# Attention units that hold two kinds of heads, in a kernel that puts attention beside a mixture of experts

## The reference

```
q, k, v = proj(xn): 16 heads of 8 numbers
idx   = clip(pos_k - pos_q, -20, 20) + 20
attn  = softmax((q.k + q.rel_k[idx]) / sqrt(8))         # 512 x 512 for each head and row
out   = (attn @ v + sum_k attn * rel_v[idx]) @ Wo.T + bo
```

## Time and profile before

| | |
|---|---|
| time, 3 runs | 2581.75, 2585.8, 2586.46 us (median 2585.8) |
| the profiled execution | 2584.21 us, its span 2582.4 us |
| attend in the span | from 282 us to 1671 us |
| busy in the whole span | PE 2293.3, DVE 1905.0, ACT 1584.7, POOL 1038.4 us |

### The profile page before, as it was taken

One profiled execution on the slowest core, in us unless ns is written; L12 is line 12 of the kernel. 1 busy time (PEld: TensorE's weight loads), 2 busy tenths in 40 slices (PEclk: granted clock), 3 DMA queues, 4 the chain that ended last, 5 costly groups with the idle time before them and its releaser, 6 DMA issues. The chain is left out here.

```text
span 2582.4 us, 102624 instructions
## 1 busy us (share of the span) xinstructions
PE 2293.3 (89%) x37544; PEld 1609.2 (62%) x37544; DVE 1905.0 (74%) x3734; ACT 1584.7 (61%) x3954; POOL 1038.4 (40%) x1350
## 2 busy tenths in 40 slices
PE   5773599999999999999998999869999996999999
PEld 3441477767767677677676777646666664666665
DVE  5663488878878788788787888637676764777777
ACT  3442477778777777777777777637777772232322
POOL 5664445545554555455445554300000002333332
PEclk9886799999999999999999999959999997999999
DMA  6887345544544455455444554300010101101010
GB/s 191 271 271 205 87 108 120 115 108 110 122 107 111 102 124 112 106 116 123 104 115 105 121 112 105 67 25 26 24 37 24 37 25 58 37 24 37 24 37 16
DMA packets 568188, 243.42 MB, mean 94 GB/s; under 512 B 462278, under 2 KB 531526, under 8 KB 563142
## 3 DMA queue, kind: packets, MB, share of 16 engines
q1 hardware_dynamic: 567750, 237.52, 36.7%
HBM read 134.13 MB, written 103.29 MB: 92 GB/s over the span
## 5 line engine op out<-in xcount | busy, mean ns | idle before, releaser
L886 ACT ACTIVATE a_probs<-a_bank_s,a_neg_max 128x512 f32<-128x512 f32 x1024 | 694.6, 684 | 184.2 <-DVE a_neg_max L821 180.1
L821 DVE TENSOR_REDUCE a_neg_max<-a_bank_s 128x2 f32<-128x1024 f32 x512 | 627.0, 1225 | 56.0 <-ACT a_probs L886 3.7
L673 PE MATMUL a_bank_pt<-a_ident,a_probs 128*128 128x128 f32 x4096 | 573.1, 283 | 8.5 <-issue 2.6
L673 PEld LDWEIGHTS a_bank_pt<-a_ident,a_probs 128*128 128x128 f32 x4096 | 445.1, 143 | 116.4 <-issue 79.1
L866 ACT ACTIVATE a_probs_t<-a_bank_pt 128x512 f32<-128x512 f32 x512 | 305.9, 597 | 201.4 <-PE a_bank_pt L673 196.0
L807 DVE COPY a_probs_t<-a_bank_pt 128x512 f32<-128x512 f32 x512 | 350.1, 684 | 32.4 <-PE a_bank_pt L673 24.5
L662 PE MATMUL a_bank_s<-a_k,a_q 48*32 48x512 bf16 (+15 forms) x4096 | 274.1, 290 | 94.0 <-DMA a_kl<-scr_parts 65.0
L699 PE MATMUL a_bank_o<-a_probs_t,a_v 128*32 128x32 f32 (+2 forms) x15872 | 305.8, 228 | 2.0 <-issue 2.0
L699 PEld LDWEIGHTS a_bank_o<-a_probs_t,a_v 128*32 128x32 f32 x15872 | 245.8, 112 | 58.8 <-ACT a_probs_t L866 48.4
L662 PE MATMUL a_bank_s<-a_kl,a_q 48*32 48x204 bf16 (+14 forms) x3840 | 241.4, 266 | 23.6 <-ACT a_probs L886 19.1
L800 DVE TENSOR_TENSOR a_bank_s<-a_bank_s,a_win 128x144 f32<-128x144 f32 (+2 forms) x640 | 164.2, 275 | 125.9 <-PE a_bank_s L662 113.1
(11 more groups left out here) (161 smaller groups left out, 3600.1 us busy)
## 6 DMA issues: line engine op xcount, KB each, us to landing
scr_probs<-a_probs SPq DMA_DIRECT2D x256, 144.0 KB, 5.2
a_raw<-scr_qr SPq DMA_DIRECT2D x256, 96.0 KB
scr_qr<-p_qr SPq DMA_DIRECT2D x64, 320.0 KB, 2.9
a_feat<-scr_probs SPq DMA_DIRECT2D x256, 78.0 KB
scr_parts<-p_sp SPq DMA_DIRECT2D x144, 128.0 KB, 2.9
a_left<-scr_probs SPq DMA_DIRECT2D x256, 64.0 KB, 2.5
a_q<-scr_parts SPq DMA_DIRECT2D x32, 192.0 KB
a_k<-scr_parts SPq DMA_DIRECT2D x32, 192.0 KB
```

What stands on the lines that cost most here:

```text
L673: ins = nc.tensor.transpose(b_pt[bank_of(job)][:, 0, t * P:(t + 1) * P], probs[(u - 1) % 4][:, j, MAX_REL + t * P:MAX_REL + (t + 1) * P], ...
L821: nc.vector.tensor_reduce(neg_max[:, 2 * pair:2 * pair + 2], b_s[:, 2 * pair:2 * pair + 2, :], AX.X, ALU.max, negate=True).then_inc(max_ok, 1)
L886: nc.scalar.activation(probs[u % 4][:, j, MAX_REL:MAX_REL + S], b_s[:, j, :], ACT.Exp, bias=neg_max[:, j:j + 1], accum_out=sums[:, t, j, u ...
```

## The change

In a unit, blocks 0 and 1 keep the heads u % 4, and blocks 2 and 3 take the heads u % 4 ^ 1, which have the other parity (`head_of`). The banks are reordered (`PLACES`): banks 0, 1, 2, 3 hold blocks 0, 2, 1, 3, so the two banks of a pair have heads of different parity. `scores` goes over both banks with `KL` and then over both with `K`; the number and the shapes of its matmuls stay. `attended` can no longer join blocks 1 and 2 in a part. `add_window`, the sums and the store follow the new places; the store of a unit becomes two stores of two blocks each (i = 0 and i = 2), and the waits on `p_out` count 32 instead of 16. The two units of a pair (u % 4 of 0 and 1, of 2 and 3) together still cover the same heads and blocks.

```diff
+PLACES = (0, 2, 1, 3)
+def head_of(u, i):
+    return u % 4 ^ i // 2
...
-                    sp.wait_ge(p_out[k], b * 16 * NT + 16 * (u // 4))
+                    sp.wait_ge(p_out[k], b * 32 * NT + 32 * (u // 4))
...
-                    at = PROBS_AT[t % 2] + u % 4 * NJ * QBLK * WIN
-                    own = probs[u % 4][:, 0, t * P:]
-                    sp.dma_start(bass.AP(scr["probs"].tensor, at, [[WIN, P], [H * QBLK * WIN, NQB], [1, WIN]]),
-                                 bass.AP(own.tensor, own.offset, [own.ap[0], [S + 2 * MAX_REL + QBLK, NQB], [1, WIN]])
-                                 ).then_inc(p_out[u % 4], 16)
+                    for i in (0, 2):
+                        at = PROBS_AT[t % 2] + (i * H + head_of(u, i) * NJ) * QBLK * WIN
+                        own = probs[u % 4][:, PLACES.index(i), t * P + i * QBLK:]
+                        sp.dma_start(bass.AP(scr["probs"].tensor, at, [[WIN, P], [H * QBLK * WIN, 2], [1, WIN]]),
+                                     bass.AP(own.tensor, own.offset,
+                                             [own.ap[0], [2 * (S + 2 * MAX_REL) + QBLK, 2], [1, WIN]])
+                                     ).then_inc(p_out[u % 4], 16)
...
-                par = slice((u % 2) * HALF, (u % 2) * HALF + ROWS)
-                for i in pair:
-                    at = u // 4 * P + i * QBLK
-                    edge = max(at - MAX_REL, 0)
-                    for keys, a, z in ((KL, 0, edge), (K, edge, S)):
+                for right in range(2):
+                    for p in pair:
+                        i = PLACES[p]
+                        at = u // 4 * P + i * QBLK
+                        edge = max(at - MAX_REL, 0)
+                        keys, a, z = (K, edge, S) if right else (KL, 0, edge)
                         if a == z:
                             continue
+                        par = head_of(u, i) % 2 * HALF
                         for g in range(NJ):
-                            half = (NJ * g + u % 4) // 2
-                            ins = nc.tensor.matmul(b_s[g * QBLK:(g + 1) * QBLK, i, a:z], Q[s][par, half, at:at + QBLK],
-                                                   keys[s][par, half, a:z], start=a == 0, stop=z == S,
+                            half = (NJ * g + head_of(u, i)) // 2
+                            ins = nc.tensor.matmul(b_s[g * QBLK:(g + 1) * QBLK, p, a:z],
+                                                   Q[s][par:par + ROWS, half, at:at + QBLK],
+                                                   keys[s][par:par + ROWS, half, a:z], start=a == 0, stop=z == S,
...
-                        parts = [(n * QBLK, (n + 1) * QBLK, EDGES.index(max(n * QBLK - MAX_REL, 0)))
-                                 for n in range(NQB)]
+                        parts = [(n, n + 1, EDGES.index(max(n * QBLK - MAX_REL, 0))) for n in range(NQB)]
                     elif kt == t - 1:
-                        parts = [(0, QBLK, EDGES.index(P - MAX_REL)), (QBLK, P, EDGES.index(P))]
+                        parts = [(0, 1, EDGES.index(P - MAX_REL)), (1, 2, EDGES.index(P)), (2, 4, EDGES.index(P))]
                     else:
-                        parts = [(0, P, EDGES.index(P if kt < t else 0))]
+                        parts = [(n, n + 2, EDGES.index(P if kt < t else 0)) for n in (0, 2)]
                     for lo, hi, edge in parts:
+                        p, hh = PLACES.index(lo), head_of(u, lo)
...
-                                                   probs_t[u % 2][:, lo // QBLK:hi // QBLK,
+                                                   probs_t[u % 2][:, p:p + 2 * (hi - lo) - 1:2,
                                                                   kt * P + j * QBLK:kt * P + (j + 1) * QBLK],
...
-                    near = bass.AP(whole.tensor, whole.offset, [whole.ap[0], [S + QBLK, n], [1, z - a]])
-                    ins = nc.vector.tensor_tensor(near, near, win[t % 2][:, i:i + n, hh, a - edge:z - edge], ALU.add)
+                    near = bass.AP(whole.tensor, whole.offset, [whole.ap[0], [S + 2 * QBLK, n], [1, z - a]])
+                    step = (2 * NJ + head_of(u, 2) - head_of(u, 0)) * WIN
+                    ins = nc.vector.tensor_tensor(near, near, bass.AP(own.tensor, own.offset, [own.ap[0], [step, n], [1, z - a]]),
+                                                  ALU.add)
```

More of the change, by code:

```diff
@@ L678, in attended @@
             def attended(b, u, s):
-                t, hh = u // 4, u % 4
+                t = u // 4
                 after = (b, u + 1) if u < UNITS - 1 else (b + 1, 0)
@@ L686, in attended @@
                     need(pe, o_ev, b, 1, 0)
-                first = hh == 0
+                first = u % 4 == 0
                 for kt in range(NT):
                     if kt == t:
-                        parts = [(n * QBLK, (n + 1) * QBLK, EDGES.index(max(n * QBLK - MAX_REL, 0)))
-                                 for n in range(NQB)]
+                        parts = [(n, n + 1, EDGES.index(max(n * QBLK - MAX_REL, 0))) for n in range(NQB)]
                     elif kt == t - 1:
-                        parts = [(0, QBLK, EDGES.index(P - MAX_REL)), (QBLK, P, EDGES.index(P))]
+                        parts = [(0, 1, EDGES.index(P - MAX_REL)), (1, 2, EDGES.index(P)), (2, 4, EDGES.index(P))]
                     else:
-                        parts = [(0, P, EDGES.index(P if kt < t else 0))]
+                        parts = [(n, n + 2, EDGES.index(P if kt < t else 0)) for n in (0, 2)]
                     for lo, hi, edge in parts:
+                        p, hh = PLACES.index(lo), head_of(u, lo)
                         for j in range(NJ):
-                            out = b_o[32 * j:32 * j + 32, 0, t * P + lo:t * P + hi].rearrange("p (i q) -> p i q", q=QBLK)
-                            ins = nc.tensor.matmul(out, V[s][:, V_SLOTS.index((edge, kt)), j, hh * 24:hh * 24 + 32],
-                                                   probs_t[u % 2][:, lo // QBLK:hi // QBLK,
+                            out = b_o[32 * j:32 * j + 32, 0, t * P + lo * QBLK:t * P + hi * QBLK]
+                            ins = nc.tensor.matmul(out.rearrange("p (i q) -> p i q", q=QBLK),
+                                                   V[s][:, V_SLOTS.index((edge, kt)), j, hh * 24:hh * 24 + 32],
+                                                   probs_t[u % 2][:, p:p + 2 * (hi - lo) - 1:2,
                                                                   kt * P + j * QBLK:kt * P + (j + 1) * QBLK],
@@ L791, in add_window @@
             def add_window(u, pair):
-                t, hh = u // 4, u % 4
+                t = u // 4
                 first, last = t == 0 and pair == 0, t == NT - 1 and pair == 1
-                for i, n in ((0, 1), (1, 1)) if first or last else ((0, 2),):
-                    i += 2 * pair
+                for k, n in ((0, 1), (1, 1)) if first or last else ((0, 2),):
+                    p = 2 * pair + k
+                    i = PLACES[p]
                     edge = t * P + i * QBLK - MAX_REL
                     a, z = max(edge, 0), min(edge + WIN, S)
-                    whole = b_s[:, i, a:z]
-                    near = bass.AP(whole.tensor, whole.offset, [whole.ap[0], [S + QBLK, n], [1, z - a]])
-                    ins = nc.vector.tensor_tensor(near, near, win[t % 2][:, i:i + n, hh, a - edge:z - edge], ALU.add)
+                    whole, own = b_s[:, p, a:z], win[t % 2][:, i, head_of(u, i), a - edge:z - edge]
+                    near = bass.AP(whole.tensor, whole.offset, [whole.ap[0], [S + 2 * QBLK, n], [1, z - a]])
+                    step = (2 * NJ + head_of(u, 2) - head_of(u, 0)) * WIN
+                    ins = nc.vector.tensor_tensor(near, near, bass.AP(own.tensor, own.offset, [own.ap[0], [step, n], [1, z - a]]),
+                                                  ALU.add)
                 return ins
@@ L877, in row @@
                         act.wait_ge(max_ok, b * 2 * UNITS + 2 * u + pair + 1)
-                        need(act, p_out[u % 4], b, 16 * NT, 16 * t)
+                        need(act, p_out[u % 4], b, 32 * NT, 32 * t)
                         if u % 4 == 0:
@@ L886, in row @@
                             nc.scalar.activation(probs[u % 4][:, j, MAX_REL:MAX_REL + S], b_s[:, j, :], ACT.Exp,
-                                                 bias=neg_max[:, j:j + 1], accum_out=sums[:, t, j, u % 4:u % 4 + 1]
+                                                 bias=neg_max[:, j:j + 1], accum_out=sums[:, t, PLACES[j], head_of(u, PLACES[j]):head_of(u, PLACES[j]) + 1]
                                                  ).then_inc(exp_ok, 1)
```

## The result

The changed kernel takes 2717.3 us (median of 4 runs, 2696.5 to 2719.7), the kernel before on the same chip 2584.4 (2581.8 to 2586.5). The ratio is 1.050, with a 95% interval of 1.044 to 1.055: 133 us slower, where 27 us less were forecast and 2590 was the upper end of the range. The profiled execution took 2719.7 us. In kernel.py after the change the lines of attend are scores L674, transposes L686, product with V L712, the add L816, DVE's copy L824, reduction L838, L854 for `last_t`; on ACT the copy L883 and the exponentials L903.

What follows compares the result with a forecast made beforehand. DVE was taken as nearly full in attend, the change paying only where DVE waits for PE's scores. Terms -25.6, -5.8, -3.6 and +7.7 summed to -27.3: 2556.9 us profiled, 2558 as median; likeliest 2540 to 2572, range 2535 to 2590.

Steps and rivals of the forecast that it cites:

- Product with V, 0.04 us a unit: PE's product with V in attend: 24 more short instructions a unit were to add 0.04 us.
- The range's upper bound, 17 ns times 24 = 0.41: Product with V: most the 24 added instructions could cost a unit, at the mean time of a whole instruction.
- V goes by instructions: Rival, product with V: 24 more instructions at 17 ns each cost 0.41 us a unit, total 2596 us; chance 0.08.
- strong form: Same rival on the product with V, each instruction at 25 ns: 0.6 us a unit, +28, total 2614 us.
- Scores, 0.55 to 0.33 us a pair: Scores on PE: two banks in different row halves stream together, saving 0.22 us a pair.
- weigh units: Units after which (u % 4 == 1) DVE waits 0.83 us for scores: 64 gain 0.40 us each, -25.6.
- units 3 and 11: Units of a row where late transposes delay DVE's last copy: 32 in all gain 0.18 us each, -5.8.
- feature units: Units with u % 4 == 0, after which DVE waits for L721, not for scores: gain 0.
- The budget: DVE's waits for the scores before the add, 82 times, 73.8 us in all, from which the change could pay.
- Key load at the starts of rows, +7.7: Seven row starts wait for a key load that SP's second stores delay by 0.9 us: 7 x 1.1 us lost.
- I am wrong if ... the step of DVE changes in units where it had no gap: Failure sign in attend: DVE-bound units such as 10 and 14 were to stay at 4.29 us.
- two thirds of 0.12: Share of the rival that SP's queue eats the gain (2572 to 2585 us, chance 0.12) counted as faster.

Runs made afterwards that it cites:

- e4_old_parts: Changed kernel with the old, larger parts of the product with V; fast scores and two stores stay: 2563.3 us.
- e1_halves: Kernel before with only the new order and row halves of the scores: 2563.0 us.
- e3_one_store: Changed kernel with one store a unit, as before, in place of two: 2720.2 us.
- e2_split: Kernel before with only the product with V split into the smaller parts: 2763.1 us.

## Why the prediction was wrong, step by step

- **Product with V, 0.04 us a unit: this step failed.** As a time of execution it is right (1.13 us for 88 against 1.10 for 64). The step took the execution for the whole price. 44 part matmuls in place of 32 are 48 instructions more a unit, and those cost 154 us in all (after against e4_old_parts), 0.60 a unit, by PE running dry. The range's upper bound, 17 ns times 24 = 0.41, was worked out from execution too and did not hold it.
- **The rival "V goes by instructions" (0.08)** had the right part and sign, and the 0.6 us a unit of its strong form is even the mean that was measured. That is luck: its total, 2614, is 103 us short, since it let the price count in 96 of the 256 units only, and its mechanism is not the one at work. The 25 ns from start to start that the Trainium skill gives (TensorE: Matmul & The Clock Gate, section "Wait — 56ns, not 53.3ns?") are not seen: 88 in 1.13 us is 13 ns. And the loss isn't spread over the units but falls on those where a block ends.
- **Scores, 0.55 to 0.33 us a pair:** measured 0.34. Right. e1_halves gains 22.8 us and e4_old_parts 22.4; the sum had -27.3.
- **Where the gain falls: near in sum, partly by luck, and off in its parts.** By e4_old_parts' steps, weigh units (1, 5, 13) give 0.20, not 0.40; units 3 and 11 give 0.36, not 0.18; the feature units (4, 8, 12), set at 0, give 0.2 to 0.4; units 2, 10 and 14 stay at 4.30 to 4.34, as forecast. Over units 1 to 14 it is 2.0 us a row, and over the whole row 1.2 (mean of 15 rows, 86.4 to 85.2).
- **The budget was misread too.** The 0.83 us before the add stand after units 1, 5 and 13, in 45 places and not 64. After unit 9 DVE waits for `project` instead, and then 0.23 us for the scores:

```profile
DVE a_y_in L849 <- PE a_bank_pt L747: 17.4, 15, 1.2
```

The wait before the add, which was to fall from 73.8 to about 45 us, rose to 80.7 in e4_old_parts (300 to 1650 us): it fell by 0.19 after those units and grew at the starts of rows, from 1.5 to 3.5 us (median):

```profile
DVE a_bank_s L816 <- PE a_bank_s L674: 80.7, 64, 5.9
```

- **Key load at the starts of rows, +7.7:** the direction was right, the size too small. The wait rose by 21.3 us in e4_old_parts, of which 12.9 come without a second store, since PE mostly comes earlier to the same load. The store itself adds 0.50 us to SP (0.89 for two, 0.39 for one), forecast 0.45, and e3_one_store shows that in the changed kernel this costs nothing.
- **"I am wrong if ... the step of DVE changes in units where it had no gap":** that was the sign. Unit 10 went from 4.30 to 5.74, its neighbour from 4.67 to 6.33. The other one, a V block over 1.3 us, came true too, at 1.73 on average.
- A slip in the chances: 0.62 + 0.10 + two thirds of 0.12 is 0.80, not 0.78. It changes nothing else.
- Nothing in the views of before showed a dry engine except the starts after the branch, put down as "issue". The row that could have warned is queue 8 with 282 packets, beside 64 matmuls and their loads in 1.10 us.

What stays open: when exactly a block's packet is asked for. That it starts near the end of the block before where the gaps are long is read from the counts above; what makes it start there, and some 185 instructions ahead in before, was not tested. Also why e2_split (8.7 us a row dry, 99.0 us a row) is slower than after (12.4 and 95.8): the slow scores explain some 22 of the 46 us, and its granted clock is lower (0.922 against 0.935 over the span), but neither was tried apart.

## What to carry to other kernels

When a change adds instructions to a stretch in which the engine already runs short ones, count them against the block of 256 as well as against the engine. Here some 200 instructions that take 1.5 us left it dry for up to 2.8 us, and the same added ones in two halves cost a fifth (33 us for 154). In an unrolled loop compare the instructions of one period with 256; if they nearly agree, every period meets the boundary at one place, and a few instructions ahead of the loop can move it (here 2573 to 2654 us). And measure an added part alone before believing its price, since a time per instruction read inside a block says nothing of what feeds it.

## What was new about the hardware

- Instructions reach PE in packets of 16 KB, 1.1 us each (nine in ten between 0.9 and 1.6); where it had run dry for over 1 us in after, the engine went on 2.2 us after the start of one at the earliest, and 2.6 in the median.
- 32-column matmuls with their own weight loads, in four column groups, went by at 17 ns (64 in 1.10 us) and 13 ns (88 in 1.13). Idle weight loads of 48 rows and 32 columns, all into one place, took 20 ns each.
- Two bf16 streams of 48 rows in different row halves, banks apart, ran side by side: 0.34 us a pair for 0.55.
